# Turns of the identity on an otherwise waiting TensorE in the last batch's second layer of a two-layer graph attention kernel

## The chip, the cores and the metric

The kernel runs on one core of a Trainium2 chip. A core has a TensorE (PE in the profile), which multiplies a stationary operand by a moving one and writes to banks of the accumulator memory (PSUM, 2 KB per partition in each of eight banks), a VectorE (DVE), a ScalarE (ACT), a GpSimd (POOL) and a SyncE (SP), which here only issues transfers.
## What is computed

Sixteen graphs (batches) of 512 nodes with 256 features, through two layers. The first is an 8-head masked attention with a residual and a layer norm, the second a single-head graph attention whose logits are a sum of a row part and a column part:

```python
# layer 0, for each batch
q, k, v = (proj(Wq, bq), proj(Wk, bk), proj(Wv, bv))          # 8 heads of 32
scores = jnp.einsum('bhqd,bhkd->bhqk', q, k) / np.sqrt(D_HEAD)
mask = adj + jnp.eye(n, dtype=adj.dtype)[None] > 0
attn = jax.nn.softmax(jnp.where(mask[:, None], scores, -jnp.inf), axis=-1)
out = jnp.einsum('bhqk,bhkd->bhqd', attn, v)  # heads joined
h = x + out @ Wo.T + bo
x1 = (h - mu) * jax.lax.rsqrt(var + EPS) * gamma + beta
# layer 1, for each batch
feat_proj = jnp.einsum('bnh,oh->bno', x1, fc_w) + fc_b
logits = q1 + jnp.swapaxes(k1, 2, 1)          # q1, k1: feat_proj times one vector each, plus a bias
masked = logits + (1.0 - adj_mat) * NEG_INF
masked = jnp.where(masked >= 0, masked, LEAKY_SLOPE * masked)
out = jnp.einsum('bnm,bmh->bnh', jax.nn.softmax(masked, axis=-1), feat_proj) + x1
```

## The kernel before

Everything is 32-bit. Node rows lie in four groups of 128 (`NT = 4`), features in two (`DT = 2`). Layer 0 of a batch is 32 tiles (`TILES`), one for each head and group of 128 queries: a 128x512 score matmul into one of three `sm_bank` (line 529), a masked minimum on VectorE (line 975), an exponential on ScalarE (line 731), and three tiles later a turn (transposition) of the four 128x128 blocks into `et_bank` (line 539), whose copy feeds the product with `v` (line 475).

The work of a batch is spread over a software pipeline. `program` runs the iterations t = -1 to 17, each with 32 slots s. In each slot an engine does the tile's own work of batch t, and beside it the steps that are due: `PE_AT`, `ACT_AT`, `DVE_AT`, `POOL_AT` and `SP_AT` give each named step an offset in slots from the start of its batch, so a step with offset 50 runs in slot 18 of the next iteration. Within a slot the order is that of the `if` lines. Layer 1 of a batch thus runs beside layer 0 of the next. Batch 15 is the last: in iteration 16 there is no further layer 0, and its second half stands alone at the end of the program.

The steps that matter here, in TensorE's order, for batch 15:

- `op1`, `op0` (offsets 44, 46): the output projection, 24 matmuls of 256 columns, through `three_terms` (each product is made of three of high and low parts, line 420). Their results are added to h and normed: VectorE adds (line 927), takes statistics (933, 939), GpSimd makes the scale and shift (1073, 1069, 1077, 1081), ScalarE writes the normed rows (715).
- `ht1`, `ht0` (offset 50): `turn_h`, four turns each (line 484), which wait for all normed rows. ScalarE copies the results to `split_hi` (669), VectorE makes `split_lo` (884).
- `fc0`, `fc1` (53, 54), `kb` (56): 24 matmuls of 256 columns and 6 of 512 (line 420 again), waiting for both `split_lo`. ScalarE copies `feat` (669), VectorE makes `q_dot` (947), then four masked maxima `l_max` (958), which also wait for `kb` and for GpSimd's `l_mask` steps (1085). GpSimd has these queued behind steps that wait for both `ht` (1090, 1095).
- ScalarE applies the leaky slope (654, four times), a negated maximum (659) and the exponentials `lexp2`, `lexp3`, `lexp0`, `lexp1` (664).
- `et2`, `et3` (62), `at2` (63), `et0` (63), `at3` (64), `et1` (65), `at0` (69), `at1` (73): `turn_z`, four turns each (498), each copied back to `z` by ScalarE (669), and `attend`, four products of 256 columns each (508; the profile has two instructions for each). Then VectorE's last two sums (915) and the store.

A turn is `nc.tensor.transpose(bank, source, ident)` with `ident` the 128x128 identity in SBUF.

Of the kernel before, what the change touches and what calls it, by code (L numbers as in the profile page):

```python
# [29 lines left out]
P = 128  # L30
NB, N, D = 16, 512, 256
# [5 lines left out]
TILES = NH * NT  # L37
# [48 lines left out]
def due(at, name, s, t):  # L86

    b = t - at[name] // TILES
    return b if at[name] % TILES == s and 0 <= b < NB else None
# [7 lines left out]
def on(t, off):  # L97

    return 0 <= t + off < NB
# [41 lines left out]
def build(nc, x, adj, wq, bq, wk, bk, wv, bv, wo, bo, gamma, beta, fc_w, fc_b, q_w, q_b, k_w, k_b, out):  # L141
    with ExitStack() as ctx:
        def sb(name, shape, dt=F32):
            return ctx.enter_context(nc.sbuf_tensor(name, shape, dt))

        def sem(name):
            return ctx.enter_context(nc.semaphore(name))
# [18 lines left out]
        ident = sb("ident", [P, P])  # L166
# [46 lines left out]
        def pb(name):  # L213
            return ctx.enter_context(nc.psum_tensor(name, [P, 512], F32))
        sm_bank = [pb(f"sm_bank{i}") for i in range(SCORED)]
# [9 lines left out]
        exp_done = Signal(sem("exp_done"), tiles)  # L225
# [138 lines left out]
        def _(pe):  # L364
# [36 lines left out]
            def bank_read(name, b):  # L401

                t, n = b + PE_AT[name] // TILES, FILLS.index(name)
                while True:
                    n, t = (n - 1, t) if n else (len(FILLS) - 1, t - 1)
                    if BANK[FILLS[n]] != BANK[name]:
                        continue
                    before = t - PE_AT[FILLS[n]] // TILES
                    if 0 <= before < NB or t < FIRST:  # L410
                        break
                who, reader = READ_BY[FILLS[n]]
                return made[who].sem, made[who].all(reader, before) if reader == "l_max" else made[who].of(reader, before)
# [17 lines left out]
            def project_qk(name, w, g, b):  # L431
                pe.wait_ge(dve_done.sem, dve_done.all("x_lo", b))
                pe.wait_ge(*bank_read(f"{name}{g}", b))
                bank = bank_of[f"{name}{g}"]
                o = slice(g * P, (g + 1) * P)
                three_terms(bank[:, :], lambda kt: ((weight_hi[:, w, kt, o], weight_lo[:, w, kt, o]),
                                                    (xt_hi[:, kt, :], xt_lo[:, kt, :]))).then_inc(pe_done.sem, 1)
# [16 lines left out]
            def out_project(half, b):  # L454
                pe.wait_ge(pool_done.sem, pool_done.all("o_lo", b))
                rows_times("op", half, o_hi, o_lo, WO, b)
# [5 lines left out]
            def times_v(k, b):  # L462
# [13 lines left out]
                                                e_t[:, k % 2, kt, i, :], start=(kt == 0), stop=(kt == NT - 1))  # L476
                last.then_inc(pe_done.sem, 1)

            def turn_h(kt, b):
                pe.wait_ge(act_done.sem, act_done.all("hn", b))  # L480
                pe.wait_ge(*bank_read(f"ht{kt}", b))
                bank = bank_of[f"ht{kt}"]
                for c in range(NT):
                    last = nc.tensor.transpose(bank[:, c * P:(c + 1) * P], h[b % 2][:, c, kt * P:(kt + 1) * P], ident[:, :])  # L484
                last.then_inc(pe_done.sem, 1)
# [7 lines left out]
            def turn_z(c, b):  # L493
                pe.wait_ge(act_done.sem, act_done.of(f"lexp{c}", b))
                pe.wait_ge(*bank_read(f"et{c}", b))
                bank = bank_of[f"et{c}"]
                for k in range(NT):
                    last = nc.tensor.transpose(bank[:, k * P:(k + 1) * P], z[:, c, k * P:(k + 1) * P], ident[:, :])  # L498
                last.then_inc(pe_done.sem, 1)

            def attend(c, b):
                k = c % 2
                pe.wait_ge(act_done.sem, max(act_done.of(f"et{c}", b), act_done.all("feat", b)))
                if k == 0:
                    pe.wait_ge(*bank_read(f"at{c}", b))
                bank = bank_of[f"at{c}"]
                for kt in range(NT):
                    last = nc.tensor.matmul(bank[:, k * D:(k + 1) * D], z[:, c, kt * P:(kt + 1) * P], feat[:, kt, :],  # L508
                                            start=(kt == 0), stop=(kt == NT - 1))
                last.then_inc(pe_done.sem, 1)  # L510
# [31 lines left out]
            def iteration(t):  # L542
                for s in range(TILES):
                    if t == FIRST and s == FIRST_QK:
                        pe.wait_ge(setup_dve, 3)
                    if t == FIRST and s == AFTER_QK:
                        other_weights()
                    if t == 0 and s == 0:
                        pe.wait_ge(setup_act, 7)
                        pe.wait_ge(setup_dve, 10)  # L550
                    if (b := due(PE_AT, "at3", s, t)) is not None:
                        attend(3, b)
                    if (b := due(PE_AT, "et1", s, t)) is not None:
                        turn_z(1, b)
                    if (b := due(PE_AT, "q0", s, t)) is not None:
                        project_qk("q", WQ, 0, b)
                    if (b := due(PE_AT, "rb0", s, t)) is not None:
                        spread_recip(0, b)
                    if (b := due(PE_AT, "pv2", s, t)) is not None:
                        times_v(2, b)  # L560
                    if (b := due(PE_AT, "et2", s, t)) is not None:
                        turn_z(2, b)
                    if (b := due(PE_AT, "at2", s, t)) is not None:
                        attend(2, b)
                    if on(t, 0):
                        scores(s, t)
                    if (b := due(PE_AT, "k1", s, t)) is not None:
                        project_qk("k", WK, 1, b)
                    if (b := due(PE_AT, "rb1", s, t)) is not None:
                        spread_recip(1, b)  # L570
                    if (b := due(PE_AT, "at1", s, t)) is not None:
                        attend(1, b)
                    if (b := due(PE_AT, "op1", s, t)) is not None:
                        out_project(1, b)
                    if (b := due(PE_AT, "xt0", s, t)) is not None:
                        turn_x(0, b)
                    if (b := due(PE_AT, "op0", s, t)) is not None:
                        out_project(0, b)
                    if (b := due(PE_AT, "ht1", s, t)) is not None:
                        turn_h(1, b)  # L580
                    if (b := due(PE_AT, "fc0", s, t)) is not None:
                        fc_project(0, b)
                    if (b := due(PE_AT, "fc1", s, t)) is not None:
                        fc_project(1, b)
                    if (b := due(PE_AT, "kb", s, t)) is not None:
                        key_logits(b)
                    if (b := due(PE_AT, "q1", s, t)) is not None:
                        project_qk("q", WQ, 1, b)
                    u, off = ago(s, TURN)
                    if on(t, off):  # L590
                        turn(u, t + off)
                    if (b := due(PE_AT, "pv3", s, t)) is not None:
                        times_v(3, b)
                    if (b := due(PE_AT, "at0", s, t)) is not None:
                        attend(0, b)
                    if (b := due(PE_AT, "v1", s, t)) is not None:
                        value_project(1, b)
                    if (b := due(PE_AT, "v0", s, t)) is not None:
                        value_project(0, b)
                    if (b := due(PE_AT, "xt1", s, t)) is not None:  # L600
                        turn_x(1, b)
                    if (b := due(PE_AT, "k0", s, t)) is not None:
                        project_qk("k", WK, 0, b)
                    if (b := due(PE_AT, "pv0", s, t)) is not None:
                        times_v(0, b)
                    if (b := due(PE_AT, "ht0", s, t)) is not None:
                        turn_h(0, b)
                    if (b := due(PE_AT, "pv1", s, t)) is not None:
                        times_v(1, b)
                    if (b := due(PE_AT, "et3", s, t)) is not None:  # L610
                        turn_z(3, b)
                    if (b := due(PE_AT, "et0", s, t)) is not None:
                        turn_z(0, b)
# [576 lines left out]
```

## Time and profile before

| | us |
|---|---|
| median of three runs | 969.0 (968.88 to 969.69) |
| the profiled execution, its whole time | 967.68 |
| its span, first to last instruction | 965.4 |
| TensorE busy in the span | 929.8 (96%) |
| ScalarE busy | 796.7 (83%) |
| VectorE busy | 768.6 (80%) |
| GpSimd busy | 300.4 (31%) |
| mean granted TensorE clock | 0.988 |

The span is what the trace covers; 2.3 us of the execution lie around it. A busy share is an average over the whole run and says little of the last 40 us, in which the engines work one behind the other. Times in the trace count from the span's start.

### The profile page before, as it was taken

Reading aid. Unit: us, or ns where it says so; the run is one execution under the profiler, and the core shown is the slowest. Engines: PE = TensorE matmul, PEld = TensorE weight load, DVE = VectorE, ACT = ScalarE, POOL = GpSimd, SP = SyncE. Lnnn points to the kernel's source line nnn. Section 1 sums busy time; section 2 is a strip of 40 time slices with the busy share of each in tenths; the row PEclk is TensorE's granted clock in tenths of the full one; section 3 lists DMA queues with packets and bytes.
Section 4 is the critical chain, followed back from the end, with each engine's and each line's share of the span. In section 5 each row is a group of like instructions: output and inputs, shape, how many; then the busy total and the mean of one; then the engine's idle time right before and its main releaser. Section 6 shows DMA issues by size and latency. Waiting matters only on the chain. (4 is left out here: it accounts for less than half of the span.)

```text
span 965.4 us, 22082 instructions
## 1 busy us (share of the span) xinstructions
PE 929.8 (96%) x7432; PEld 776.6 (80%) x7432; DVE 768.6 (80%) x2012; ACT 796.7 (83%) x1900; POOL 300.4 (31%) x408
## 2 busy tenths in 40 slices
PE   5889999999999999999999999999999999999966
PEld 4668788788878878888887888888788888887854
DVE  4687979788797988879788887978879797887832
ACT  3768989889897998989888897988889798887923
POOL 0012334323243431424342142433223343322441
PEclk9999999999999999999999999999999999999988
DMA  6677767476675747666574766657467765746100
GB/s 188 140 134 130 132 106 114 128 117 150 110 132 101 117 124 117 140 120 124 111 116 120 121 127 127 118 122 117 126 112 131 130 102 134 116 110 110 44 23 22
DMA packets 74718, 112.59 MB, mean 117 GB/s; under 512 B 7024, under 2 KB 33648, under 8 KB 74608
## 3 DMA queue, kind: packets, MB, share of 16 engines
q1 hardware_dynamic: 74608, 111.18, 59.7%
q8 instruction: 62, 1.02, 0.5%
q14 instruction: 48, 0.39, 0.2%
HBM read 52.44 MB, written 8.39 MB: 63 GB/s over the span
## 5 line engine op out<-in xcount | busy, mean ns | idle before, releaser
L975 DVE CUSTOM_DVE_ANT_0 sm_bank<-sm_bank,masks 128x512 f32<-128x512 f32 x512 | 352.4, 698 | 116.9 <-PE sm_bank L529 113.2
L731 ACT ACTIVATE e<-sm_bank,row_min 128x512 f32<-128x512 f32 x512 | 356.2, 698 | 33.0 <-DVE row_min L975 33.0
L539 PE MATMUL et_bank<-ident,e 128*128 128x128 f32 x2048 | 308.5, 273 | 3.2 <-DVE e_t L983 1.9
L539 PEld LDWEIGHTS et_bank<-ident,e 128*128 128x128 f32 x2048 | 252.1, 140 | 42.2 <-issue 6.8
L529 PE MATMUL sm_bank<-k_stack,q_stack 96*128 96x512 f32 x512 | 247.7, 484 | 5.6 <-DMA k_stack<-kt_lo 3.2
L723 ACT COPY e_t<-et_bank 128x512 f32<-128x512 f32 x272 | 161.2, 593 | 17.6 <-PE et_bank L539 15.9
L983 DVE COPY e_t<-et_bank 128x512 f32<-128x512 f32 x240 | 164.4, 685 | 11.4 <-PE et_bank L539 9.8
L529 PEld LDWEIGHTS sm_bank<-k_stack,q_stack 96*128 96x128 f32 x512 | 97.0, 190 | 36.2 <-issue 26.5
L475 PE MATMUL o_bank<-e_t,v 128*32 128x256 f32 x2048 | 123.8, 382 | 0.0
L508 PE MATMUL shared<-feat,z 128*128 128x256 f32 x512 | 121.8, 381 | 0.8 <-ACT z L669 0.8
L731 ACT ACTIVATION_READ_ACCUMULATOR e<-sm_bank,row_min 128x1 f32 x512 | 107.4, 210 | 0.0
L508 PEld LDWEIGHTS shared<-feat,z 128*128 128x128 f32 x512 | 94.0, 191 | 12.5 <-ACT z L669 1.3
L475 PEld LDWEIGHTS o_bank<-e_t,v 128*32 128x32 f32 x2048 | 60.0, 109 | 43.7 <-issue 10.7
L1105 POOL TENSOR_SCALAR recip_wide<-row_recip 128x512 f32<-128x512 f32 x32 | 47.7, 1492 | 122.8 <-DVE row_recip L895 122.8
L1099 POOL TENSOR_SCALAR_AFFINE_SELECT masks<-masks 128x512 bf16<-128x512 bf16 x16 | 10.2, 638 | 229.7 <-DVE masks L964 229.7
L420 PE MATMUL shared<-weight_hi,split_hi 128*128 128x256 f32 x256 | 74.9, 292 | 1.5 <-DVE split_lo L884 1.5
L1111 POOL TENSOR_TENSOR split_lo<-o_raw,split_hi 128x512 fp32r<-128x512 f32 x32 | 40.8, 1274 | 112.2 <-ACT split_hi L706 112.2
L420 PE MATMUL shared<-weight_hi,split_lo 128*128 128x256 f32 x256 | 73.6, 287 | 0.0
L420 PE MATMUL shared<-weight_lo,split_hi 128*128 128x256 f32 x256 | 73.4, 287 | 0.0
L975 DVE DVE_READ_ACCUMULATOR2_ANT row_min<- 128x1 f32 x512 | 72.7, 142 | 0.0
L669 ACT COPY z<-shared 128x512 f32<-128x512 f32 x64 | 37.8, 590 | 31.4 <-PE shared L498 31.4
L420 PE MATMUL shared<-xt_hi,weight_hi 128*128 128x512 f32 x128 | 53.5, 418 | 1.6 <-DVE xt_lo L884 1.6
(112 smaller groups left out, 1576.6 us busy)
## 6 DMA issues: line engine op xcount, KB each, us to landing
adj_in<-in_adj SPq DMA_DIRECT2D x32, 1024.0 KB, 5.5
q_stack<-qt_hi SPq DMA_DIRECT2D x62, 256.0 KB, 8.0
k_stack<-kt_hi SPq DMA_DIRECT2D x62, 256.0 KB, 7.8
x_in<-in_x SPq DMA_DIRECT2D x16, 512.0 KB, 6.4
h<-in_x SPq DMA_DIRECT2D x16, 512.0 KB, 3.8
out_y<-h SPq DMA_DIRECT2D x32, 256.0 KB, 6.7
q_stack<-qt_lo SPq DMA_DIRECT2D x31, 256.0 KB, 7.1
k_stack<-kt_lo SPq DMA_DIRECT2D x31, 256.0 KB, 11.1
```

What stands on the lines that cost most here:

```text
L420: last = nc.tensor.matmul(bank, a, b, start=(kt == 0 and n == 0), stop=(kt == kts - 1 and n == 2))
L475: last = nc.tensor.matmul(o_bank[i * DH:(i + 1) * DH, 2 * half * P:2 * (half + 1) * P], v[:, kt, o:o + DH], e_t[:, k % 2, kt, i, :], start ...
L508: last = nc.tensor.matmul(bank[:, k * D:(k + 1) * D], z[:, c, kt * P:(kt + 1) * P], feat[:, kt, :], start=(kt == 0), stop=(kt == NT - 1))
L529: nc.tensor.matmul(sm_bank[(TILES * b + s) % SCORED][:, :], q_stack[g][:, i, qt * P:(qt + 1) * P], k_stack[g][:, i, :], start=True, stop=T ...
L539: last = nc.tensor.transpose(et_bank[n % TURNED][:, c * P:(c + 1) * P], e[:, n % ROOM, c * P:(c + 1) * P], ident[:, :])
L669: nc.scalar.copy(dst, bank_ap).then_inc(act_done.sem, 1)
L723: nc.scalar.copy(turned_to(u), et_bank[(TILES * b + u) % TURNED][:, :].rearrange("p (c n) -> p c n", c=NT)).then_inc(act_copied.sem, 1)
L731: nc.scalar.activation(e[:, k, :], sm_bank[n % SCORED][:, :], ACT.Exp, scale=-1.0, bias=row_min[:, k:k + 1], accum_out=row_sum[:, g, qt, i ...
L975: nc.vector.tensor_tensor_reduce(bank[:, :], bank[:, :], mask[b % 2][:, qt * N:(qt + 1) * N], 1.0, -LOWEST, ALU.add, ALU.min, row_min[:, k ...
L983: nc.vector.tensor_copy(turned_to(u), et_bank[(TILES * b + u) % TURNED][:, :].rearrange("p (c n) -> p c n", c=NT))\
L1105: nc.gpsimd.tensor_scalar(recip_wide[g][:, :].rearrange("p (k d) -> p k d", d=DH), row_recip[:, g, :, :].rearrange("p q i -> p (q i)").uns ...
L1111: nc.gpsimd.tensor_tensor(o_lo[:, g, :], o_raw[g][:, :], f(o_hi[:, g, :]), ALU.subtract).then_inc(done, 1)
```

## The change

A function `bridge(n, b)` is added to TensorE's program. For every batch but the last it does nothing. For batch 15 it waits until ScalarE's exponentials of all tiles of the batch are done and then issues n turns of `ident` itself into the first 128 columns of `sm_bank[0]`, a bank that nothing reads after the last tile. It is called in two places: with 46 turns ahead of `turn_h(1, b)`, and with 38 turns ahead of `turn_z(2, b)`. No other engine's program changes.

```diff
+            def bridge(n, b):
+                if b < NB - 1:
+                    return
+                pe.wait_ge(exp_done.sem, exp_done.of(TILES - 1, b))
+                for _ in range(n):
+                    nc.tensor.transpose(sm_bank[0][:, 0:P], ident[:, :], ident[:, :])
+
             def turn_h(kt, b):
...
                     if (b := due(PE_AT, "et2", s, t)) is not None:
+                        bridge(38, b)
                         turn_z(2, b)
...
                     if (b := due(PE_AT, "ht1", s, t)) is not None:
+                        bridge(46, b)
                         turn_h(1, b)
```

On TensorE, between the output projection and the turns of h of batch 15, the program before has in a row (`split_hi`, `split_lo` are the two parts of the layer's input, `shared` the two banks that the side steps use):

```order
L420 MATMUL shared<-weight_lo,split_hi 128x256
L420 MATMUL shared<-weight_hi,split_lo 128x256
L484 MATMUL shared<-ident,h 128x128 x8
L420 MATMUL shared<-weight_hi,split_hi 128x256
L420 MATMUL shared<-weight_lo,split_hi 128x256
```

and the changed one (lines from 484 on are seven or more higher there, since the new function stands ahead of them):

```order
L420 MATMUL shared<-weight_lo,split_hi 128x256
L420 MATMUL shared<-weight_hi,split_lo 128x256
L484 MATMUL sm_bank<-ident 128x128 x46
L491 MATMUL shared<-ident,h 128x128 x8
L420 MATMUL shared<-weight_hi,split_hi 128x256
L420 MATMUL shared<-weight_lo,split_hi 128x256
```

The 46 turns stand between the last matmul of the output projection and the first turn of h; nothing else moved.

On TensorE, from the last matmul of `kb` to the end of the program, the program before has (`uk_lo` is the folded key vector's low part, `z` the attention rows, `feat` the projected features):

```order
L420 MATMUL shared<-split_hi,uk_lo 128x512
L498 MATMUL shared<-ident,z 128x128 x8
L508 MATMUL shared<-feat,z 128x256 x4
L498 MATMUL shared<-ident,z 128x128 x4
L508 MATMUL shared<-feat,z 128x256 x4
L498 MATMUL shared<-ident,z 128x128 x4
L508 MATMUL shared<-feat,z 128x256 x8
```

and the changed one:

```order
L420 MATMUL shared<-split_hi,uk_lo 128x512
L484 MATMUL sm_bank<-ident 128x128 x38
L505 MATMUL shared<-ident,z 128x128 x8
L515 MATMUL shared<-feat,z 128x256 x4
L505 MATMUL shared<-ident,z 128x128 x4
L515 MATMUL shared<-feat,z 128x256 x4
L505 MATMUL shared<-ident,z 128x128 x4
L515 MATMUL shared<-feat,z 128x256 x8
```

The 38 turns stand ahead of the first turns of z, and the rest keeps its order.

## Rows read from the trace of the kernel before

**Rows 1.** Page, part 2: granted TensorE clock in 40 equal slices, in tenths.

```profile
PEclk9999999999999999999999999999999999999988
```

**Rows 2.** Timeline of PE, end of the program: start us, duration us, instructions, idle before.

```profile
925.41 0.47 PE L420 MATMUL shared<-weight_hi,split_hi 128*128 128x256 f32 x1
...
928.35 0.28 PE L420 MATMUL shared<-weight_hi,split_lo 128*128 128x256 f32 x1
934.62 1.97 PE L484 MATMUL shared<-ident,h 128*128 128x128 f32 x8 [5.99 <-ACT h L715]
938.14 0.55 PE L420 MATMUL shared<-weight_hi,split_hi 128*128 128x256 f32 x1 [1.55 <-DVE split_lo L884]
...
943.18 0.41 PE L420 MATMUL shared<-weight_hi,split_lo 128*128 128x256 f32 x1
...
944.59 0.40 PE L420 MATMUL shared<-split_hi,uk_lo 128*128 128x512 f32 x1
950.29 1.97 PE L498 MATMUL shared<-ident,z 128*128 128x128 f32 x8 [5.30 <-ACT z L664]
952.17 2.73 PE L508 MATMUL shared<-feat,z 128*128 128x256 f32 x8
954.74 0.60 PE L498 MATMUL shared<-ident,z 128*128 128x128 f32 x4
955.18 1.89 PE L508 MATMUL shared<-feat,z 128*128 128x256 f32 x8
...
958.27 3.69 PE L508 MATMUL shared<-feat,z 128*128 128x256 f32 x16 [0.77 <-ACT z L669]
```

**Rows 3.** Stretches: from:to, length, busy (instructions) of PE, PEld, DVE, ACT, POOL, clock, DMA.

```profile
29.00:32.00 3.00, 1.43 (x8) 1.05 (x9) 1.95 (x6) 3.00 (x9) 0.00 (x0) 1.00 0.32 93
32.00:35.00 3.00, 3.00 (x18) 3.00 (x15) 1.31 (x3) 0.80 (x3) 0.00 (x0) 0.52 1.04 246
35.00:38.00 3.00, 3.00 (x22) 2.60 (x22) 2.34 (x6) 2.46 (x6) 0.00 (x0) 0.91 1.06 161
...
932.00:934.00 2.00, 0.00 (x0) 0.00 (x0) 0.00 (x0) 1.51 (x4) 0.38 (x2) 0.81 0.00 0
...
938.00:943.00 5.00, 4.86 (x23) 4.89 (x24) 0.90 (x4) 0.59 (x1) 4.59 (x8) 0.50 0.00 0
943.00:946.00 3.00, 1.99 (x9) 1.39 (x8) 1.66 (x7) 0.59 (x1) 1.55 (x3) 0.92 0.00 0
946.00:948.00 2.00, 0.00 (x0) 0.00 (x0) 1.77 (x6) 1.41 (x3) 0.00 (x0) 0.73 0.00 0
...
953.00:958.00 5.00, 4.51 (x23) 3.65 (x22) 1.05 (x3) 2.34 (x6) 0.00 (x0) 0.93 0.01 3
```

**Rows 4.** Timelines of ACT, DVE and POOL at the end of the program.

```profile
936.68 0.59 ACT L669 CAST split_hi<-shared 128x512 fp32r<-128x512 f32 x1 [0.27 <-PE shared L484]
937.30 0.69 DVE L884 TENSOR_TENSOR split_lo<-shared,split_hi 128x512 fp32r<-128x512 f32 x1 [0.16 <-ACT split_hi L669]
941.05 1.31 POOL L1085 TENSOR_SCALAR adj_in<-adj_in 128x512 f32<-128x512 f32 x2
945.24 0.69 DVE L958 CUSTOM_DVE_ANT_0 z<-shared,adj_in 128x512 f32<-128x512 f32 x1
950.14 0.71 ACT L664 ACTIVATE z<-z,l_negmax 128x512 f32<-128x512 f32 x1
951.44 0.59 ACT L669 COPY z<-shared 128x512 f32<-128x512 f32 x1 [0.50 <-PE shared L498]
```

**Rows 5.** Timeline of PE at the start: the first matmuls of the program.

```profile
4.56 1.94 PE L371 MATMUL sm_bank<-ident,z 128*128 128x128 f32 x8 [4.56 <-DMA z<-in_L_gnn_Wk]
```

**Rows 6.** Line 428, up to 9 us: duration ns min/median/max, first and last start.

```profile
L428 PE MATMUL shared<-ident,x_in x8: 273/421/477, 6.7 to 8.3; 128*128 128x128 f32 x8
```

**Rows 7.** Timeline of PE, two other places: a turn group behind a pause, and narrow matmuls.

```profile
31.51 0.51 PE L529 MATMUL sm_bank<-k_stack,q_stack 96*128 96x512 f32 x1 [1.49 <-DMA k_stack<-kt_lo]
...
920.18 1.93 PE L475 MATMUL o_bank<-e_t,v 128*32 128x256 f32 x32
```

## The prediction

> **What bounds the kernel now.** I read four views in this order. The page's clock slices [rows 1] come first: TensorE's granted clock is at full level nearly everywhere and under it in the last two slices. The timeline of PE at the end of the program [rows 2] shows why: after the last score tile the engines work one behind the other, and TensorE pauses for 5.99 us (the layer norm) before the turns of h, 1.55 us before the `fc` products, 5.30 us (maxima, slope, exponentials) before the turns of z, and 0.77 us before the last products. The stretches [rows 3] place the clock: 0.81 over 932 to 934 means that it fell from 2.4 to 1.2 GHz at 933.2; 0.50 up to 943, and 0.92 over 943 to 946, mean that it came back at 943.5; 0.73 over 946 to 948 that it fell again at 946.9, some 2.1 us after TensorE's last work; 0.93 over 953 to 958 that it came back at 953.7. The other engines' rows [rows 4] show who hands work to TensorE in between. TensorE's work of those 17 low us lies on the chain that sets the end; its pauses do too, but they belong to the other engines, and the change leaves them.
>
> So nothing is bought by the added turns themselves. What they can buy is that the real work after a pause runs at 2.4 GHz.
>
> **What is added, and whether it fits.** 84 turns, no other engine touched; the semaphore that `bridge` waits for has long been reached, so I cost the wait at nothing. Spacing of turns at full clock: four turns of z begin at 954.74 and the next instruction at 955.18 [rows 2], 0.11 us each. At the low clock eight take 1.97 us [rows 2], of which the last takes 0.42 by itself [rows 6]: 1.55 / 7 = 0.22 each. The ends: 0.06 us, as for the narrow matmuls, 32 in 1.93 us [rows 7], and 0.22. I take 0.11, the same operation at the clock that is granted when both groups begin.
>
> First group: TensorE is free at 928.35 + 0.12 = 928.47; 46 x 0.11 = 5.1 us, to 933.5. The turns of h can't start before 934.62 (they wait for the normed rows), so 1.1 us of cover are left and nothing is delayed. Second group: free at 944.59 + 0.23 = 944.82; 38 x 0.11 = 4.2 us against a pause to 950.29, 1.3 us left. Both places shift together with the rest if the first group brings something.
>
> **Do such turns hold the clock?** At the start of the program the recorded clock doesn't tell, but the durations do: TensorE's first work is eight turns at low-clock size, 1.94 us against the 1.97 us above [rows 5], then comes the second group of eight turns, which begins at 421 to 477 ns and ends with 273 ns [rows 6]. TensorE had done nothing but turns when its clock rose. I take it that turns count as work. The Trainium skill says otherwise (TensorE: Matmul & The Clock Gate, Part 4: PE-mode transpose: in transpose mode the full clock doesn't engage, since it doesn't count as busy in the same way). By that rule the sum below would be nought for both pauses, and the case is priced as a rival. The trace's first rows speak against it. What they leave open is that here both operands are the identity, mostly zeros.
>
> **First pause, worked out.** With the clock held through it, the turns of h give their first half after 0.60 us (as four turns take at 954.74, [rows 2]) and both after 1.04. ScalarE's two copies of 0.62 us run from 935.26 to 936.5, VectorE's two subtractions of 0.69 follow from 935.88 to 937.26 (both sizes from [rows 4]), and the `fc` products start at 937.40 in place of 938.14: 0.74 us. The 24 products up to `fc1` last from 938.14 to 943.18 + 0.41 = 943.59, 5.45 us; the same 24 of the output projection, at full clock, last from 925.41 to 928.35 + 0.28, 3.22 us [rows 2]. All at full clock they would give 2.23 us. The maxima follow `fc1` by a copy and two dot products at fixed distance, up to 945.24 [rows 4].
>
> I don't expect all of that. After the added turns TensorE still has a pause of 1.1 us, 0.9 us of turns, and a pause of some 1.9 us (935.5 to 937.4) that is ScalarE's and VectorE's and that nothing fills. At 946.9 the clock fell 2.1 us after the last work; at 32.1 (0.52 over 32 to 35, [rows 3]) it fell 0.6 us into new work that had been preceded by a pause of 1.49 us [rows 7]. So I forecast a new fall between 936 and 938, late enough for the turns of h. The low stretch that began at 32.1, with full work behind it, ended at 35.5 (0.91 over 35 to 38, [rows 3]): 3.4 us. Beginning up to 0.7 us before the products, it would cover 2.7 to 3.4 us of them. At the low clock a product costs 5.04 / 23 = 0.219 us, at the full one 2.94 / 23 = 0.128, so each low us loses 0.42: 1.1 to 1.4 us, I take 1.3. Left of the first pause: 0.74 + 2.23 - 1.3 = 1.7 us.
>
> What is late next: the maxima also wait for `kb` and GpSimd's masks. The masks end at 941.05 + 1.31 = 942.36 [rows 4]; they are queued behind the turns of h and come 0.9 us earlier with them, at 941.4, while the maxima would start at 945.24 - 1.7 = 943.5. `kb` ends 0.3 us ahead of the maxima before and stays about there. No new bound.
>
> **Second pause, worked out.** Times here are those of before; all come 1.7 us earlier. At full clock the turns of z for `et2` are done at 950.9, those for `et3` wait for the second exponential (950.14 + 0.71, plus its accumulator read, some 950.94; [rows 4]) and end at 951.5. The copy of `et2` stands behind that exponential too, so it runs from 950.98 to 951.6 in place of 951.44 to 952.03 [rows 4], and `at2` starts at 951.62 in place of 952.17: 0.55 us. Its eight instructions take 1.89 us, as `at3` at 955.18, in place of 2.73 [rows 2]: 0.84 us. The rest was at full clock already. Sum: 1.4 us. The pause that is left, 1.3 us with full work ahead of it, is shorter than those of 1.49 and 2.1 us behind which the clock fell, so I expect it to hold.
>
> **Sum.** 1.7 + 1.4 = 3.1 us. Against the profiled execution's own time, 967.68, that is 964.6 (its span 965.4 becomes 962.3). The median of the runs shown is 1.3 us above the profiled execution, 969.0, within a spread of 0.8: 969.0 - 3.1 = 965.9.
>
> **Rivals.** (a) The clock holds everywhere, or falls only for a moment: 0.74 + 2.23 + 1.39 = 4.4 us, 964.6. For it: no pause over 2 us is left. Against it: the two pauses around the short turns of h lie close together. Chance 14%. (b) The first pause goes as forecast, but the clock falls once more in or just after the second, whose 1.3 us and the short waits between the turns of z make thin work; or it stays low through all of `fc` and `kb`, as it did for 10.2 us before. Either takes about 1.4 us from the sum: 1.3 to 2.0 us are left, 967.3. Chance 17%. (c) The change doesn't do what it says: the identity's turns follow each other at 0.06 us, the groups end after 2.8 and 2.3 us, and pauses of over 3 us bring the clock down as before: 969.0, 5%. (d) **Slower**: the turns don't hold the clock, or the clock is low when the second group starts, and the group then holds up the turns of z behind it. With the clock of before, 19 turns fit between 944.82 and 946.9, and the other 19 take 0.22 each, to 951.1: 0.8 us late, nothing gained, 969.8. With all 38 at the low level the group ends at 944.8 + 8.4 = 953.2, 2.9 us late, 971.9. It decides for "slower" when 30 or more of the 38 run at 1.2 GHz (38 x 0.11 + 30 x 0.11 is 1.9 us more than the pause of 5.47). Against it: [rows 6]. Chance 9%, a third of it over the mark. This is also where the skill's rule of above would lead.
>
> **How the numbers follow.** The forecast has 55%. About 0.2%, 1.9 us, is what a measurement of this kernel can tell from no change. Faster by more: 53 of the forecast's 55, all 14 of (a), 6 of the 17 of (b), 73%. Slower: 3%. The rest, 24%, is within. The range: down to (a) less half a us of spread between executions, 964.1; up to the weak end of (b), 969.0 - 1.3 = 967.7. Outside lie (c), (d) and little else, some 16%.
>
> **What would show it.** In the profile after: 46 turns from 928.5 to 933.5 and 38 behind `kb`, each with a pause of about 1 us behind it; the turns of h in about 1.0 us rather than 1.97; a stretch of clock 0.50 of about 3.4 us starting at 936 to 938 and none later; `fc` products with both sizes, 0.41 and 0.28; the turns of z and `at2` at 0.27 and at full size, `at2` in 1.89 us; the end 3.1 us earlier. The prediction is wrong if the turns of h last 1.97 us (turns of the identity don't hold the clock), if the turns of z start right behind the 38th added turn (the group is too long), or if the maxima wait for GpSimd.

## The result, and the profile after

| | before | after |
|---|---|---|
| median of five runs, us | 969.69 (968.88 to 971.25) | 964.55 (964.19 to 966.23) |
| the profiled execution, us | 967.68 | 964.55 |
| its span, us | 965.4 | 962.4 |
| its mean granted clock | 0.988 | 0.992 |

The ratio is 0.995, with a 95% interval from 0.9938 to 0.9963: 3.6 to 6.0 us faster. The changed kernel, run once more at another time, gave 0.9957 (0.9945 to 0.997). All ratios are of fast runs alone; one execution of all those below, of `kb_bank`, was slow (1180 us) and is left out. The time of 964.55 lies inside the range of the prediction (964.1 to 967.7), near its lower end; the direction was right, and the gain is larger than the 3.1 us forecast, which lies below the interval. The profiled execution came close to rival (a): the clock stayed at its full level from the output projection to TensorE's last product.

The timeline of PE after, end of the program (start us, duration us, instructions, idle before; lines from 484 on are seven or nine higher than before), answers to [rows 2]:

```profile
926.20 0.47 PE L420 MATMUL shared<-weight_hi,split_hi 128*128 128x256 f32 x1
...
929.13 0.28 PE L420 MATMUL shared<-weight_hi,split_lo 128*128 128x256 f32 x1
929.26 5.18 PE L484 MATMUL sm_bank<-ident 128*128 128x128 f32 x46
935.41 1.09 PE L491 MATMUL shared<-ident,h 128*128 128x128 f32 x8 [0.97 <-ACT h L724]
938.21 0.35 PE L420 MATMUL shared<-weight_hi,split_hi 128*128 128x256 f32 x1 [1.71 <-DVE split_lo L893]
...
941.03 0.28 PE L420 MATMUL shared<-weight_hi,split_lo 128*128 128x256 f32 x1
941.64 0.47 PE L420 MATMUL shared<-split_hi,uk_hi 128*128 128x512 f32 x1 [0.32 <-DVE q_dot L956]
...
943.10 4.31 PE L484 MATMUL sm_bank<-ident 128*128 128x128 f32 x38
948.45 1.36 PE L505 MATMUL shared<-ident,z 128*128 128x128 f32 x8 [1.04 <-ACT z L673]
949.87 1.97 PE L515 MATMUL shared<-feat,z 128*128 128x256 f32 x8
951.67 0.60 PE L505 MATMUL shared<-ident,z 128*128 128x128 f32 x4
...
955.21 3.69 PE L515 MATMUL shared<-feat,z 128*128 128x256 f32 x16 [0.77 <-ACT z L678]
```

The 46 turns take 5.18 us and leave 0.97 us before the turns of h; the 38 take 4.31 and leave 1.04. The turns of h last 1.09 us where they lasted 1.97, and no fc product has the low-clock size of 0.41. The stretches (from:to, length, busy of PE, PEld, DVE, ACT, POOL, granted clock, DMA), against [rows 3]:

```profile
934.00:938.00 4.00, 1.53 (x13) 1.05 (x10) 1.23 (x2) 2.43 (x5) 1.42 (x3) 1.00 0.00 0
938.00:943.00 5.00, 4.47 (x30) 4.11 (x31) 1.85 (x9) 1.18 (x2) 4.59 (x7) 1.00 0.02 3
943.00:946.00 3.00, 3.00 (x29) 2.91 (x28) 2.53 (x8) 1.26 (x3) 1.50 (x3) 1.00 0.00 0
946.00:948.00 2.00, 1.41 (x13) 1.17 (x11) 0.00 (x0) 1.94 (x5) 0.00 (x0) 1.00 0.00 0
948.00:953.00 5.00, 4.44 (x25) 3.64 (x26) 0.18 (x1) 4.27 (x11) 0.00 (x0) 1.00 0.00 0
```

Where 938 to 943 stood at 0.50 it stands at 1.00, and so does everything up to 953.

**A measure that leaves the start of the program out.** The first product of the output projection begins at 925.41 us before and at 926.20 after, though nothing ahead of it is changed. The difference arises in the first 100 us of the program. There the clock falls at different times (first at 32.1 us before and at 25.9 after; six of the twelve traces have one more fall between 73 and 75), and even the first projection product doesn't begin at one time (10.15 us before, 10.66 after, 12.39 in `third_kb`). Behind that no trace has a low stretch before the tail. Other traces below begin this product anywhere from 923.38 to 928.11. So I compare the *tail*, from that product's start to the end of the span: 965.4 - 925.41 = 40.0 us before, 962.4 - 926.20 = 36.2 after, 3.8 us of gain. It divides like this:

| piece of the tail | before | after | gain | forecast |
|---|---|---|---|---|
| first product to the turns of h | 9.21 | 9.21 | 0 | 0 |
| turns of h to the first fc product | 3.52 | 2.80 | 0.72 | 0.74 |
| the 24 fc products | 5.45 | 3.10 | 2.35 | 0.93 (2.23 less 1.3) |
| their end to the first maximum | 1.65 | 2.09 | -0.44 | 0 |
| first maximum to the turns of z | 5.05 | 5.05 | 0 | 0 |
| turns of z to `at2` | 1.88 | 1.42 | 0.46 | 0.55 |
| `at2` to the next turns | 2.57 | 1.80 | 0.77 | 0.84 |
| the rest, to the end | 10.66 | 10.73 | -0.07 | 0 |

Two pieces differ from the forecast by more than 0.1 us: the fc products, and what follows them. VectorE's timeline after shows the second, against the 945.24 of [rows 4], where the first maximum followed its dot product at once:

```profile
942.44 0.48 DVE L956 CUSTOM_DVE_ANT_0 z<-shared,qw_row,logit_bias 128x256 f32<-128x256 f32 x1
...
943.40 0.69 DVE L967 CUSTOM_DVE_ANT_0 z<-shared,adj_in 128x512 f32<-128x512 f32 x1 [0.47 <-DVE q_dot L956]
```

VectorE stands idle for 0.47 us before the maximum. It waits for `kb`, which itself waited 0.32 us for the dot products of `fc0`: both use `shared0`, and `kb` may not write before `q_dot0` has read. The run `kb_bank` below tests this.

### The profile page after: what moved, and what is told of

It is laid out like the page before. It is cut to its first block and busy times, and to the rows that moved or that the text cites. A ratio compares the mean times of both kernels' runs of the same rounds, so it can differ in the third digit from the quotient of the medians.

```text
span 962.4 us, 22250 instructions
## 1 busy us (share of the span) xinstructions
PE 936.8 (97%) x7516; PEld 783.2 (81%) x7516; DVE 768.7 (80%) x2012; ACT 796.7 (83%) x1900; POOL 300.5 (31%) x408
```

## The experiments

The theory after the result: turns of the identity keep TensorE's clock at 2.4 GHz; each group gains by itself; whether the clock falls at the fc products is a matter of the execution; and `kb` is a new, small bound. Nine further kernels were run, and the changed one again. Diffs are against the changed kernel.

**One group at a time.** `first_only`:

```diff
-                        bridge(38, b)
```

> Only the 46 turns ahead of the turns of h are kept. Theory (turns of the identity hold the clock, and each place gains by itself): the clock stays at 1.00 through the fc and kb products and falls in the 5.3 us pause behind kb, as before. From the first product of the output projection to the end of the span it was 40.0 us before and 36.2 with both groups; with the first group alone some 37.4 (2.6 us of gain at the first place, none at the second). Rival (one group is enough, since what matters is that the clock is high when kb ends): the clock holds through the second pause too, and the stretch is 36.2. Rival (the gain is elsewhere than at these two places): 40.0.

Measured: ratio 0.9978 (0.9967 to 0.9989), tail 966.4 - 928.11 = 38.3 us.

`second_only`:

```diff
-                        bridge(46, b)
```

> Only the 38 turns ahead of the turns of z are kept. Theory: the first pause costs what it cost before (clock low over the turns of h and most fc products), then the clock is held from kb on; from the output projection's first product to the end of the span 38.8 us (1.2 of gain). If the clock is still low when the group starts, part of the 38 turns takes 0.22 us each and the turns of z start late: up to 40 us or more. Rival (the second group is worth nothing without the first): 40.0 or above.

Measured: ratio 0.9983 (0.9973 to 0.9993), tail 966.0 - 927.57 = 38.4 us. The timelines of PE, first group alone:

```profile
937.33 1.09 PE L491 MATMUL shared<-ident,h 128*128 128x128 f32 x8 [0.98 <-ACT h L723]
...
950.35 1.97 PE L505 MATMUL shared<-ident,z 128*128 128x128 f32 x8 [5.18 <-ACT z L672]
952.23 3.64 PE L515 MATMUL shared<-feat,z 128*128 128x256 f32 x8
```

and second group alone:

```profile
936.77 1.97 PE L491 MATMUL shared<-ident,h 128*128 128x128 f32 x8 [5.99 <-ACT h L723]
...
946.58 4.31 PE L484 MATMUL sm_bank<-ident 128*128 128x128 f32 x38
952.07 1.36 PE L505 MATMUL shared<-ident,z 128*128 128x128 f32 x8 [1.18 <-ACT z L672]
```

Each group helps the work behind its own pause. Up to the turns of z, the first alone gains 24.88 - 22.24 = 2.64 us, as both do (22.25). From the turns of z on, the second alone gains 15.11 - 13.93 = 1.18, which is the 1.2 expected; its tail is 38.4 and not 38.8 because the part ahead of its group was 24.50 us long in this trace, 0.38 shorter than before, with a clock that fell and came back 0.9 us earlier counted from the output projection. That part is not the group's doing. The rival that one group would carry the clock over both pauses falls: with the first alone the stretch behind the second pause has

```profile
950.00:955.00 5.00, 4.65 (x15) 3.83 (x16) 0.18 (x1) 3.59 (x10) 0.00 (x0) 0.50 0.01 3
```

My 37.4 us for that kernel was missed by 0.9: there `at2` ran wholly at the low clock and took 3.64 us, where before it was 2.73 since the clock came back in its middle. What an unfilled pause costs thus depends on where in the following work the clock returns.

**Too few turns.** `short` (both groups 10, as in the diff) and `less` (30 ahead of the turns of h and 24 ahead of those of z):

```diff
-                        bridge(38, b)
+                        bridge(10, b)
...
-                        bridge(46, b)
+                        bridge(10, b)
```

> Both groups cut to 10 turns, 1.1 us each, so that pauses of 5.0 and 4.3 us are left. Theory (the gain is the held clock): the clock falls in both pauses as before, the stretch from the output projection's first product to the end is within 0.5 us of the 40.0 before, no difference in time. Rival (a few turns just after the work are enough): 36.2 us and the whole gain.

> The groups are cut to 30 and 24 turns (3.3 and 2.6 us), which leaves pauses of 2.7 us before the turns of h and 2.6 us before those of z. Theory (the clock falls after pauses of about this size, since in the kernel before it fell 2.1 us after the last work): it falls at one place or both, and between a third and all of the gain is lost, 37.5 to 40 us in the stretch. Rival (pauses under 3 us are harmless): 36.2 us and the whole gain.

Measured: `short` 1.0001 (0.999 to 1.0012), tail 965.9 - 925.41 = 40.5 us; `less` 0.9992 (0.998 to 1.0003), tail 966.5 - 927.02 = 39.5 us. Both intervals include no change. So 54 of the 84 turns bring next to nothing. The timeline of PE for `less`:

```profile
936.24 1.09 PE L491 MATMUL shared<-ident,h 128*128 128x128 f32 x8 [2.72 <-ACT h L724]
939.04 0.55 PE L420 MATMUL shared<-weight_hi,split_hi 128*128 128x256 f32 x1 [1.71 <-DVE split_lo L893]
939.39 0.42 PE L420 MATMUL shared<-weight_lo,split_hi 128*128 128x256 f32 x1
```

and its stretches:

```profile
930.00:937.00 7.00, 4.28 (x40) 4.04 (x39) 2.11 (x9) 2.08 (x5) 1.66 (x4) 1.00 0.00 1
937.00:939.00 2.00, 0.33 (x4) 0.09 (x1) 1.29 (x2) 1.06 (x2) 1.58 (x3) 0.77 0.00 0
939.00:944.00 5.00, 4.96 (x23) 4.99 (x24) 0.90 (x4) 0.59 (x1) 4.59 (x8) 0.50 0.00 0
```

The clock outlived the pause of 2.72 us and the turns of h, and fell in the next pause, of 1.71 us: this is the fall that I had forecast for the changed kernel, with pauses of 0.97 and 1.71 us, and there it didn't come in the profile. In the second place the clock was at 1.00 until the turns of z began, 2.56 us behind the 24 added ones, and fell in them:

```profile
951.32 1.82 PE L505 MATMUL shared<-ident,z 128*128 128x128 f32 x8 [2.56 <-ACT z L673]
952.94 3.02 PE L515 MATMUL shared<-feat,z 128*128 128x256 f32 x8
```

and, among the stretches,

```profile
946.00:951.00 5.00, 2.76 (x25) 2.52 (x23) 2.65 (x10) 3.31 (x6) 0.00 (x0) 1.00 0.00 0
951.00:955.00 4.00, 3.68 (x13) 2.95 (x14) 0.00 (x0) 3.38 (x10) 0.00 (x0) 0.59 0.00 0
```

**Too many turns.** `long_second`:

```diff
-                        bridge(38, b)
+                        bridge(76, b)
```

> The second group is doubled to 76 turns. Theory (turns are spaced 0.11 us and only the pause covers them): the group of 38 left 1.04 us of cover, 38 more take 4.3 us, so the turns of z start 3.2 us later than with both groups as changed; the first half of these turns' own exponentials is then long over. The stretch from the output projection's first product to the end is 36.2 + 3.2 less up to 0.5 us that the later turns and copies catch up: 38.9 to 39.4 us. Rival (TensorE isn't on the chain there): 36.2.

Measured: 0.9989 (0.9975 to 1.0003), tail 964.8 - 925.78 = 39.0 us, as expected. The timeline of PE:

```profile
942.66 8.46 PE L484 MATMUL sm_bank<-ident 128*128 128x128 f32 x76
950.96 1.04 PE L505 MATMUL shared<-ident,z 128*128 128x128 f32 x8
```

76 turns take 8.46 us, 0.11 each, and the turns of z follow without a pause, 2.9 us later than with 38. This is the danger of rival (d), made by length instead of by a low clock: what exceeds the pause is paid in full, and here it took back most of the gain (1.0 us of the tail's 3.8 is left, and the ratio's interval includes no change).

**Do turns of nothing but the identity raise a low clock?** `prewarm_after`:

```diff
+            for _ in range(12):
+                nc.tensor.transpose(et_bank[0][:, 0:P], ident[:, :], ident[:, :])
             pe.wait_ge(qk_loaded, 16 * N_QK)
             turn_weight(WQ)
```

> The changed kernel, and 12 turns of the identity at the very start of TensorE's program, while it waits for the first weights (to 4.56 us). Theory (turns of the identity raise a low clock as other turns do): the eight turns of the first weights, 1.94 us at the low clock, run partly or wholly at 0.27 us each, and the first products start up to 1.5 us earlier; of this at most 1 us reaches the end, since the loads bind soon after. Rival (the identity, mostly zeros, doesn't count, and the clock was held by something else): the first eight turns last 1.94 us.

Measured: 0.995 (0.9932 to 0.9968), the same as the change. The timeline of PE at the start, against [rows 5]:

```profile
1.58 2.82 PE L376 MATMUL et_bank<-ident 128*128 128x128 f32 x12 [1.58 <-POOL minus_half L1067]
4.36 1.23 PE L371 MATMUL sm_bank<-ident,z 128*128 128x128 f32 x8
6.63 1.09 PE L430 MATMUL shared<-ident,x_in 128*128 128x128 f32 x8 [1.04 <-DMA x_in<-in_x]
10.06 0.47 PE L422 MATMUL shared<-xt_hi,weight_hi 128*128 128x512 f32 x1 [2.34 <-DVE xt_lo L895]
```

The eight turns of the first weights take 1.23 us in place of 1.94, with nothing ahead of them but turns of the identity. In the other traces these eight take 1.94. So turns of the identity do raise the clock, and the trace disagrees with the Trainium skill (TensorE: Matmul & The Clock Gate, Part 4: PE-mode transpose), by which they would not. (The profile calls every turn MATMUL; it doesn't show in which mode of the engine a turn ran.) No time comes of it: the turns of x then wait 1.04 us for their load, and the first product starts at 10.06, before at 10.15, not up to 1.5 us earlier.

This trace shows more at its end. Its tail has the same code as the changed kernel's, but the clock fell in it. The stretches:

```profile
933.00:935.00 2.00, 1.09 (x8) 0.86 (x8) 0.38 (x1) 1.20 (x3) 0.57 (x1) 1.00 0.00 0
935.00:937.00 2.00, 0.95 (x6) 0.98 (x7) 0.91 (x2) 0.07 (x1) 1.92 (x4) 0.88 0.00 0
937.00:939.00 2.00, 2.00 (x11) 2.00 (x10) 0.00 (x0) 0.34 (x1) 1.84 (x4) 0.50 0.03 8
939.00:941.00 2.00, 2.00 (x13) 1.91 (x13) 0.90 (x4) 0.50 (x2) 1.84 (x4) 0.76 0.00 0
```

0.88 over 935 to 937 is a fall at 936.5, half a us into the fc products; it came back at 940. That is nearly the forecast's case: a low stretch of 3.4 us that covers the products, here from 0.5 us behind their start rather than from ahead of it. The tail is 961.3 - 924.03 = 37.3 us in place of 36.2; the forecast's gain of 3.1 us would have given 36.9. The products and the first maximum behind them:

```profile
936.05 0.36 PE L422 MATMUL shared<-weight_hi,split_hi 128*128 128x256 f32 x1 [1.71 <-DVE split_lo L895]
...
940.38 0.28 PE L422 MATMUL shared<-weight_hi,split_lo 128*128 128x256 f32 x1
...
942.30 0.69 DVE L969 CUSTOM_DVE_ANT_0 z<-shared,adj_in 128x512 f32<-128x512 f32 x1
```

The 24 products last 4.61 us, 1.51 more than the 3.10 of the changed kernel, so the fall costs a little more than the 1.3 of the forecast. But the maximum now starts 1.64 us behind them without a wait, as before the change (1.65), and not 2.09: the slow products hide the wait for `kb`. The tail is thus only 1.1 us longer.

**The pause that is left, and the bank.** `third`:

```diff
                     if (b := due(PE_AT, "fc0", s, t)) is not None:
+                        bridge(13, b)
                         fc_project(0, b)
```

> Both groups as changed, and a third of 13 turns of the identity ahead of the first fc product, in the pause of 1.7 us after the turns of h that nothing filled. Theory (that pause doesn't bring the clock down, it is too short): nothing changes, 36.2 us from the output projection's first product to the end, the ratio of the change (0.995). Rival, the forecast's: in some executions the clock does fall there, and the third group takes this away: up to 1.3 us more in the runs' median (0.9937), with the fastest runs unchanged.

Measured: 0.9942 (0.9925 to 0.9959), tail 959.6 - 923.38 = 36.2 us. The pause between the turns of h and the products shrinks to 0.29 us, and a tail in which the clock held anyway doesn't change. Whether the runs gain is not shown: 0.9942 is under the change's 0.995 and 0.9957, but the intervals overlap.

`kb_bank`:

```diff
-                pe.wait_ge(*bank_read("kb", b))
+                if b < NB - 1:
+                    pe.wait_ge(*bank_read("kb", b))
...
+        def kb_bank(b):
+            return bank_of["kb"] if b < NB - 1 else sm_bank[1]
```

with `kb_bank(b)` in place of `bank_of["kb"]` in `key_logits` and `layer1_maxima`.

> Both groups as changed; in the last batch kb writes to sm_bank 1 instead of the shared bank that it shares with fc0, so it no longer waits for the two dot products that read that bank. Theory (in the changed kernel kb is late because of this bank, 0.3 us of waiting behind 0.3 us of products, and the maxima wait for kb): the first maximum starts 0.5 us earlier, right behind the last dot product, and the stretch is 35.7 us. Rival (GpSimd's masks, which end about 1 us before the maxima, or the dot products bind at once): under 0.2 us.

Measured: 0.9953 (0.9935 to 0.997), tail 959.8 - 924.02 = 35.8 us: 0.4 us less in the trace, too little for the timing. The first maximum starts at 940.79, 1.64 us behind the last fc product (ended 939.15), as before the change, in place of 2.09: the wait was the bank's.

`third_kb` has both edits.

> Third group of 13 turns ahead of the fc products and kb in a bank of its own, together. Theory: the third group keeps the clock high in every execution (worth 1.1 us in those in which it fell there, nothing in the others), the bank is worth 0.4 us in all: 35.8 us from the output projection's first product to the end, and a median some 0.4 to 1.0 us under that of the changed kernel of the same call. Rival (the two do not add, since GpSimd's masks end where the maxima would then start): 36.2 us.

Measured: 0.9939 (0.9925 to 0.9954), tail 962.6 - 926.89 = 35.7 us. In VectorE's timeline the first maximum follows its dot product with no wait:

```profile
943.13 0.48 DVE L962 CUSTOM_DVE_ANT_0 z<-shared,qw_row,logit_bias 128x256 f32<-128x256 f32 x1
943.54 0.09 DVE L962 DVE_READ_ACCUMULATOR2_ANT q_dot<- 128x1 f32 x1
943.66 0.69 DVE L973 CUSTOM_DVE_ANT_0 z<-sm_bank,adj_in 128x512 f32<-128x512 f32 x1
```

Beside it the changed kernel ran again (`after_again`).

> The changed kernel once more, beside the one above. Theory (in some executions the clock falls around the start of the fc products, in others it does not): over the executions the mean clock takes several values, and the time spreads by 2 us or more; the profile shows a stretch of 36.2 us if the clock held and about 37.3 if it fell. Rival (it always holds in this kernel, and the fall came with the turns at the start of the program): 36.2 and no low stretch after 900 us.

Measured: 0.9957 (0.9945 to 0.997), tail 961.9 - 925.73 = 36.2 us. The two medians are 964.13 us for `third_kb` and 965.36 for the change; the 1.2 us between them are a little more than the 0.4 to 1.0 expected, and the intervals of the two ratios overlap. It is the fastest version by its ratio, and not shown faster than the change beyond measurement.

The mean clocks of the six executions of `after_again` are 0.992, 0.993, 0.996, 0.996, 0.992 and 0.999; the profiled one of 0.992 kept 1.00 over the tail, so its low stretches lie at the start. I can't tell from a mean in how many of the others the tail's clock fell. Three traces ran the whole changed tail (`after`, `after_again`, `prewarm_after`): two held, one fell. Up to the fc products `first_only`, `long_second` and `kb_bank` have the same steps on TensorE too, with the first group and the unfilled pause of 1.71 us, and in all three the products ran at full clock. That makes five held and one fallen of six traces. How often it falls, and whether the turns at the start had a part in the one fall (`after_again` fits its theory and its rival alike), stays open.

## Why the prediction was right, and where it was off

**What came and what was forecast.** The forecast's own course, with a new fall of the clock at the fc products, is not what the profile after shows; that is nearly rival (a), which had 14%. The time still fell inside the range because the range reached down to that rival. The 969.0 that the sum starts from was the median of the first three executions; with all five it is 969.69, and from there the 3.1 us would have given 966.6, 2 us above what was measured.

**What bounds the end, and what the turns can buy: right.** Short groups, which occupy TensorE and leave the clock to fall, gave 1.0001; the full ones 0.995.

**Spacing and cover: right.** 46 turns in 5.18 us and 38 in 4.31 (forecast 5.1 and 4.2), with 0.97 and 1.04 us left (1.1 and 1.3). `long_second` confirms the 0.11 us over 76 turns and that the pause is all the cover there is.

**Turns hold the clock: right.** It was inferred from [rows 5, 6]; `prewarm_after` shows it with the identity alone. Rival (d) is out for this kernel, (c) as well.

**The fall at the fc products: the term that was mis-sized.** The forecast took 1.3 us off for it. In the profile after it was 0, and so in four of the five other traces that ran these steps. The mechanism is real, as `prewarm_after` (1.51 us in the products) and `less` show, but I gave it as what happens, with 55%, and the full hold 14%. I had the two levels of the clock, one fall 1.9 us behind TensorE's last work (it ended at 944.99; the prediction's 2.1 counts from 944.82), one behind a pause of 1.49, and nothing that told how pauses of 1.0 and 1.7 us with 1.1 us of turns between them would go; a number for "sometimes" was wanted, and I put a fixed price on it. With the term at zero the sum is 4.4 us; the tail gained 3.8, and most of the difference is the next point. One small sum is off as well, to no effect: with 30 of the 38 turns at the low clock the group exceeds its pause by 7.48 - 5.47 = 2.0 us, not 1.9.

**"No new bound": wrong by 0.44 us.** I checked that `kb` would end before the maxima by moving it with the fc products, and checked GpSimd's masks, but not the bank that `kb` writes. Before, its wait for `q_dot0` was over when the slow fc products ended (`q_dot0` finished at 942.6, `kb` began at 943.39), and so no row showed it. With the products at full clock it showed, `kb_bank` gets 0.4 us of it back, and in `prewarm_after`, where the products were slow again, it was gone.

**The second pause: right to 0.16 us.** Forecast 1.39, measured 0.46 + 0.77 = 1.23.

**The level.** 3.8 us of tail are 0.39%, the ratio says 0.50% with an interval that reaches down to 0.37%. The two agree within it. The profiled execution before was among the quicker ones of its kernel (967.68 against a median of 969.69), which the prediction had bridged with the median. The low stretches come at other places in each execution: in `short` the clock came back earlier in the fc products, but `at2` ran wholly low, and its tail is 40.5 us. A typical tail of the kernel before may thus be longer than the 40.0 of its one profile; no run shows it.

## What to carry to other kernels

At the end of a kernel, where engines work one behind the other, look at the granted clock beside the timeline: matmuls at 1.2 GHz behind a wait of another engine cost time when they lie on the chain that ends last (the 24 fc products took 5.45 us in place of 3.10), and dummy turns that fill the wait take this back, if they end shortly before it does (here about 1 us). Size the group from the spacing of the same operation at the clock that it will run at; 54 of the 84 turns were worth next to nothing here, and twice as many cost 2.9 us. When a stretch becomes faster, check the buffers that its steps share as well as the waits that the trace shows: a release that came early enough before leaves no row.

## What the runs showed that I had not expected

Pauses filled to a little over half are little better than unfilled ones: `less`, with 54 of the 84 turns, is at 0.9992 where the change is at 0.995, and can't be told from no change. The clock outlived a pause of 2.72 us in `less` and then fell in a pause of 1.71 us, after 1.09 us of turns, although the same 1.71 us, behind a pause of 0.97 or 0.98, were harmless in five of six traces. What decides it isn't shown here.

The same code had tails of 36.2 and 37.3 us, and the first 100 us of the program moved its later parts by up to 4.7 us (the output projection's first product of batch 15 at 923.38 in one trace and at 928.11 in another), which is as much as the whole gain. From some 130 us to that product all traces keep step within 0.2 us. Spans of single executions (959.6 with the third group, 962.4 for the change, with equal tails of 36.2) would have told a story that isn't there; the tail, counted from an instruction behind which the programs differ, gave the same 36.2 us three times.
